# A fused attention and feed-forward block in fp32: the first feed-forward product with its rows on partitions, in place of transposes of them

## The reference, cut to what matters

```python
# x: (8, 1024, 256); every product in fp32
xn = _layernorm(x)
x_proj = silu(xn @ W1 + b1); u, v, q, k = split(x_proj, 4)        # after a second layer norm of xn
attn = silu(einsum(q, k)) / S                                     # 16 heads of 16
y = _layernorm(av * u, gamma, beta) @ W2 + b2
h = layer_norm(xn, ln1_g, ln1_b)                                  # 256 wide
h = einsum('bsd,hd->bsh', h, ternary_quant(w1)) + b1              # 1024 wide
h = layer_norm(gelu(h), ln2_g, ln2_b)
out = einsum('bsh,dh->bsd', h, ternary_quant(w2)) + b2
return x + y + out
```

## Time and profile before

| | us |
|---|---|
| median of 3 executions | 1493.01 (1492.65 to 1493.11) |
| the profiled execution | 1493.36 |
| its span, first to last instruction | 1491.6 |
| one batch, start to start | 181 |
| TensorE busy | 1464.8 (98%) |
| ScalarE busy | 1208.9 (81%) |
| VectorE busy | 895.3 (60%) |
| GpSimd busy | 97.4 (7%) |
| granted TensorE clock | 0.997 of full |

### The profile page before, as it was taken

One profiled execution on the slowest core, in us unless ns is written; L12 is line 12 of the kernel. 1 busy time (PEld: TensorE's weight loads), 2 busy tenths in 40 slices (PEclk: granted clock), 3 DMA queues, 4 the chain that ended last, 5 costly groups with the idle time before them and its releaser, 6 DMA issues.

```text
span 1491.6 us, 25963 instructions
## 1 busy us (share of the span) xinstructions
PE 1464.8 (98%) x9942; PEld 784.7 (53%) x9942; DVE 895.3 (60%) x1719; ACT 1208.9 (81%) x1273; POOL 97.4 (7%) x197
## 2 busy tenths in 40 slices
PE   8999999999999999999999999999999999999998
PEld 7445555455554555554554455545555455554544
DVE  5557655576546854468654685447755476545745
ACT  4788888888788887887878878788788887888885
POOL 2001000010000100001000010000100001000001
PEclk9999999999999999999999999999999999999999
DMA  7351052410524106340153402443033510435100
GB/s 248 81 128 57 15 132 65 130 57 15 156 71 100 58 15 156 95 104 29 30 155 99 113 1 59 126 129 84 1 89 110 142 57 5 115 81 142 29 1 29
DMA packets 67996, 123.49 MB, mean 83 GB/s; under 512 B 12832, under 2 KB 14496, under 8 KB 66976
## 3 DMA queue, kind: packets, MB, share of 16 engines
q1 hardware_dynamic: 67712, 121.57, 29.9%
q10 hardware_dynamic: 160, 0.26, 0.1%
HBM read 79.84 MB, written 41.94 MB: 82 GB/s over the span
## 4 chain that ended last, share of the span: by engine, by line
PE 88%; DVE 5%; ACT 4%; issue 1%; DVEq 1%; DMA 0%; ACTq 0%
PE outs L1101 30%; PE scores L1079 22%; PE fill L1136 10%; PE fill L1170 9%; PE fill L1154 7%; PE fill L1186 3%; PE fill L1163 3%; ACT attn L636 3%; PE fill L1145 2%; DVE tmp L917 1%; PE fill L1126 1%; DVE hid L900 1%; ACT hid L681 1%; DVE st L813 1%; ACT L636 1%
## 5 line engine op out<-in xcount | busy, mean ns | idle before, releaser
L636 ACT ACTIVATE attn<-scores 128x1024 f32<-128x1024 f32 x1024 | 991.4, 1023 | 225.3 <-PE scores L1079 220.6
L1101 PE MATMUL outs<-attn,V 128*32 128x512 f32 x4096 | 494.3, 600 | 0.0
L1079 PE MATMUL scores<-QS,KS 64*128 64x512 f32 x2048 | 387.7, 452 | 8.3 <-ACT attn L636 7.0
L1079 PEld LDWEIGHTS scores<-QS,KS 64*128 64x128 f32 x2048 | 163.0, 184 | 300.4 <-ACT attn L636 241.5
L1101 PEld LDWEIGHTS outs<-attn,V 128*32 128x32 f32 x4096 | 107.2, 109 | 235.8 <-issue 235.1
L900 DVE SCALAR_TENSOR_TENSOR hid<-fill,ratq,fb1b 128x512 f32<-128x512 f32 x128 | 96.1, 751 | 77.6 <-PE fill L1154 72.3
L917 DVE TENSOR_TENSOR tmp<-fill,l2g 128x512 f32<-128x512 f32 x128 | 88.6, 692 | 88.6 <-PE fill L1163 81.1
L1170 PE MATMUL fill<-Wq,hgh 128*128 128x256 f32 x504 | 128.2, 292 | 2.0 <-DVE hgl L924 1.1
L1136 PE MATMUL fill<-xp,W1h 128*128 128x512 f32 x384 | 128.4, 416 | 0.5 <-DVE xp L949 0.5
L1170 PE MATMUL fill<-Wq,hgl 128*128 128x256 f32 x504 | 123.1, 282 | 0.0
L1170 PEld LDWEIGHTS fill<-Wq,hgh 128*128 128x128 f32 x504 | 95.8, 190 | 18.9 <-issue 14.6
(11 more groups left out here) (138 smaller groups left out, 1349.3 us busy)
## 6 DMA issues: line engine op xcount, KB each, us to landing
QS<-q_scratch SPq DMA_DIRECT2D x254, 128.0 KB, 3.3
k_scratch<-kst SPq DMA_DIRECT2D x64, 256.0 KB
q_scratch<-qst SPq DMA_DIRECT2D x64, 256.0 KB
KS<-k_scratch SPq DMA_DIRECT2D x128, 128.0 KB, 3.2
KS<-k_scratch SPq DMA_DIRECT2D x256, 64.0 KB, 3.4
out_dram<-part SPq DMA_DIRECT2D x15, 512.0 KB, 2.6
xin<-in_x SPq DMA_DIRECT2D x7, 1024.0 KB, 5.1
xin<-in_x SPq DMA_DIRECT2D x2, 512.0 KB, 4.3
```

What stands on the lines that cost most here:

```text
L636: nc.scalar.activation(attn_of(g)[:, 2 * hf:2 * hf + 2, :], SP[:, 2 * hf:2 * hf + 2, :], ACT.Silu).then_inc(s_silu, 1)
L1079: ins = mm(SP[:, j, :], KS[rows, pair, t * P:(t + 1) * P], QS[rows, pair - c * PPC, h * HALF:(h + 1) * HALF], start=True, stop=True)
L1101: ins = mm(OP[32 * j:32 * j + 32, g // RUN % 2, :], V[:, t, c * HPC // 2 + j, o * DH:o * DH + 2 * DH], attn_of(g)[:, n, :], start=(o == 0 ...
```

## The change: what it does

1. **f1** is now `f1.h.c`, half of the tokens (512) by 128 of the 1024 hidden features. The stationary operand is a 128x128 piece of `Wq1`, the moving operand a pair of y (256 columns), so a step has 8 matmuls of 256 columns in place of 4 of 512. The product has the hidden features on partitions and the tokens along the row, as f2 wants them. The bias is a value per partition; the ratio per token can't be, so it is multiplied into y before.
2. That ratio has to lie along a row in every partition: SP writes it to DRAM (`write_ratio`) and loads it broadcast (`load_ratio`), and `y` waits for it.
3. The transposes `g` (128 in all, of four instructions), the norming `nrm2` and the moments `ln2` are gone. `hg.t.r` multiplies, rounds and subtracts as `g` did, out of SBUF.
4. The second layer norm is taken out of the product. Sums and sums of squares over the features are needed: in `sum.i` GpSimd squares and adds the 8 feature tiles of a pair (15 instructions of 128x256); the plain sum is made by VectorE in one tensor_reduce for pairs 0 and 1, and by GpSimd with 7 more instructions for pairs 2 and 3. `ts.i`: TensorE adds over the partitions with 4 fp32 matmuls of 2 columns, VectorE makes mean and variance (4 small instructions), GpSimd the root and its product with the mean (2 instructions). In `f2` VectorE adds mean times a constant row `gwb` (one more instruction) and then the product times the root.
5. **TABLE** and `LAST_ROUNDS` are made anew; the load of the next x comes earlier on SP's queue, after `px` instead of after f1; `gelu.0` and `gelu.1` lie side by side, and `gelu.2` and `gelu.3`.
6. The preparation has a product for `gwb` (8 matmul calls) and one for the bias column (24 small ones) in place of two for a bias row.

```diff
 TABLE (rounds 12 to 31, two rows joined to one round)
+12  f1.0.3 | f1.0.4 gelu.0 f1.0.5 f1.0.6 f1.0.7 f1.1.0 f1.1.1 f1.1.2 gelu.1 hg.0.0 hg.0.1
+13  sum.0 | f1.1.3
+14  f1.1.4 f1.1.5 f1.1.6 f1.1.7 | ts.0 sum.1 f2.0 gelu.2 gelu.3 hg.1.0
+15  | hg.1.1
+16  xn.0 f2.1 hg.2.0 xt.0 xn.1 | hg.2.1
+17  ts.1 xt.1 |
+18  | f2.2
+19  | hg.3.0 k.0.0 hg.3.1 xn.2
+20  q.0.0 | sum.2
+21  f2.3 | hg.4.0 hg.4.1
+22  | ts.2 sum.3 xt.2
+23  f2.4 hg.5.0 hg.5.1 |
+24  xn.3 v.0 |
+25  v.1 |
+26  v.2 xt.3 |
+27  f2.5 |
+28  hg.6.0 hg.6.1 k.0.1 | ts.3
+29  f2.6 | hg.7.0
+30  v.3 hg.7.1 |
+31  q.0.1 | f2.7 vs.0
...
 SP, body(b)
+                    load_ratio(b)
...
+                    if h == 0 and b < NB - 1:
+                        sp.wait_ge(s_px, b + 1)
+                        load_x(b + 1)
...
-                    wait_evacuated(sp, b, ("f1", T - 3, 1))
-                    load_x(b + 1)
+                    write_ratio(b + 1)
...
 GpSimd
+                elif kind == "sum":
+                    i = a[0]
+                    pool.wait_ge(s_gelu, NP * x + i // 2 * 2 + 2)
+                    if x or i:
+                        wait_filled(pool, *((x, ("ts", i - 1)) if i else (x - 1, ("ts", NP - 1))))
+                    rows = hid_pair(i)
+                    nc.gpsimd.tensor_tensor(acc[:, 1, :], rows[:, 0, :], rows[:, 0, :], ALU.mult)
+                    if i not in SUMMED_BY_DVE:
+                        nc.gpsimd.tensor_tensor(acc[:, 0, :], rows[:, 0, :], rows[:, 1, :], ALU.add)
+                    for c in range(1, HC):
+                        nc.gpsimd.tensor_tensor(sq[:, :], rows[:, c, :], rows[:, c, :], ALU.mult)
+                        if i not in SUMMED_BY_DVE and c > 1:
+                            nc.gpsimd.tensor_tensor(acc[:, 0, :], acc[:, 0, :], rows[:, c, :], ALU.add)
+                        pool.drain()
+                        ins = nc.gpsimd.tensor_tensor(acc[:, 1, :], acc[:, 1, :], sq[:, :], ALU.add)
+                        pool.drain()
+                    ins.then_inc(s_sq, 1)
...
 VectorE
+                        V_.tensor_reduce(acc[:, 0, :], hid_pair(i).rearrange("p c n -> p n c"), mybir.AxisListType.X,
+                                         ALU.add).then_inc(s_sum, 1)
...
                     V_.tensor_tensor(tmp[:, :].rearrange("p (c n) -> p c n", n=P),
-                                     FP[:, k, :].rearrange("p (c n) -> p c n", n=P),
+                                     hid_pair(t // 2)[:, 4 * r:4 * r + 4, t % 2 * P:(t % 2 + 1) * P],
                                      l2g[:, 4 * r:4 * r + 4].unsqueeze(2).broadcast_to([P, 4, P]), ALU.mult)
...
                 elif kind == "f2":
                     t = a[0]
+                    dve.wait_ge(s_rs2, NP * x + t // 2 + 1)
+                    V_.scalar_tensor_tensor(out=part[:, t, :], in0=gwb[:, :], scalar=nm2[:, t:t + 1],
+                                            in1=part[:, t, :], op0=ALU.mult, op1=ALU.add)
...
 TensorE
-                    passes = [(part, kc) for kc in range(DC) for part in range(2)]
-                    for n, (part, kc) in enumerate(passes):
-                        ins = mm(bank, y_of(t // 2)[:, part, kc, t % 2 * P:(t % 2 + 1) * P], Wq1[:, kc, hf * HALF:(hf + 1) * HALF],
-                                 start=n == 0, stop=n == len(passes) - 1)
-                elif kind == "g":
...
+                    passes = [(kc, part) for kc in range(DC) for part in range(2)]
+                    for i in range(2):
+                        for n, (kc, part) in enumerate(passes):
+                            ins = mm(bank[:, i * PAIR:(i + 1) * PAIR], Wq1[:, kc, c * P:(c + 1) * P],
+                                     y_of(2 * h + i)[:, part, kc, :], start=n == 0, stop=n == len(passes) - 1)
+                elif kind == "ts":
+                    i = a[0]
+                    if i in SUMMED_BY_DVE:
+                        pe.wait_ge(s_sum, len(SUMMED_BY_DVE) * x + SUMMED_BY_DVE.index(i) + 1)
+                    pe.wait_ge(s_sq, NP * x + i + 1)
+                    for n in range(2):
+                        for j in range(2):
+                            col = 4 * n + 2 * j
+                            ins = mm(bank[:, col:col + 2], acc[:, n, j * P:(j + 1) * P], mean_of[:, :],
+                                     start=True, stop=True)
```

More of the change, by code:

```diff
@@ L77 @@
     "",
-    "",
-    "k.1.1",
-    "q.1.1",
-    "",
[L82 to L96, removed]
+    "u.1.1 y.1",
+    "k.1.1 y.0",
+    "ln1 y.2",
+    "q.1.1",
+    "u.0.1",
+    "u.1.0",
+    "f1.0.0 y.3",
+    "",
+    "f1.0.1 f1.0.2",
+    "f1.0.3",
+    "f1.0.4 gelu.0 f1.0.5 f1.0.6 f1.0.7 f1.1.0 f1.1.1 f1.1.2 gelu.1 hg.0.0 hg.0.1",
+    "sum.0",
+    "f1.1.3",
+    "f1.1.4 f1.1.5 f1.1.6 f1.1.7",
+    "ts.0 sum.1 f2.0 gelu.2 gelu.3 hg.1.0",
+    "",
+    "hg.1.1",
+    "xn.0 f2.1 hg.2.0 xt.0 xn.1",
+    "hg.2.1",
+    "ts.1 xt.1",
     "",
     "",
-    "ln1 g.2.1 f1.7.1",
+    "f2.2",
     "",
[L101 to L104, removed]
-    "",
-    "g.4.0 g.4.1",
-    "xt.1",
-    "xn.2 f2.4 xt.2",
-    "",
-    "k.0.0",
-    "g.5.0",
-    "g.5.1 gelu.3 v.0 xn.3 v.1",
+    "hg.3.0 k.0.0 hg.3.1 xn.2",
+    "q.0.0",
+    "sum.2",
+    "f2.3",
+    "hg.4.0 hg.4.1",
+    "",
+    "ts.2 sum.3 xt.2",
+    "f2.4 hg.5.0 hg.5.1",
+    "",
+    "xn.3 v.0",
+    "",
+    "v.1",
+    "",
+    "v.2 xt.3",
+    "",
     "f2.5",
[L114 to L117, removed]
-    "",
-    "k.0.1 g.6.1",
-    "q.0.1",
[L121 to L125, removed]
+    "",
+    "hg.6.0 hg.6.1 k.0.1",
+    "ts.3",
+    "f2.6",
+    "hg.7.0",
+    "v.3 hg.7.1",
+    "",
+    "q.0.1",
+    "f2.7 vs.0",
 )
@@ L138 @@
 LAST_ROUNDS = {
[L139 to L150, removed]
+    16: "f2.1 hg.2.0 hg.2.1",
+    17: "ts.1",
+    18: "f2.2",
+    19: "hg.3.0 hg.3.1",
+    20: "sum.2",
+    21: "f2.3 hg.4.0 hg.4.1",
+    22: "ts.2 sum.3",
+    23: "f2.4 hg.5.0 hg.5.1",
+    24: "",
+    25: "zs.0 zt.0 zt.1",
+    26: "a.0",
+    27: "f2.5 zs.1",
+    28: "hg.6.0 hg.6.1 ts.3 a.1",
+    29: "f2.6 hg.7.0",
+    30: "hg.7.1",
     31: "",
@@ L439, in last_z @@
         def last_z(i, part, c):
-            return yX[:, i, part, c, :]
+            return y01[:, i, part, c, :]
         def last_uz(i, c):
@@ L544, in _ @@
                 load_k(0, 0, h, o)
+            write_ratio(0)
             load_q(0, 0, 0, 1)
@@ L547, in _ @@
                 load_q(0, 0, 1, o)
+            load_ratio(0)
             for b in range(NB):
@@ L601, in step @@
             def step(x, kind, *a):
-                if kind in ("zt", "ln2", "ln1"):
+                if kind in ("zt", "sum", "ts", "ln1"):
                     pool.drain()
@@ L769, in setup_scales @@
                 V_.reciprocal(cq[:, :], scl[:, :])
+                dve.drain()
             def setup_ternary(raw, q, scale):
@@ L1023, in finish @@
                     dve.drain()
+                dve.wait_ge(s_rs2, NP * NB)
+                V_.scalar_tensor_tensor(out=part[:, T - 1, :], in0=gwb[:, :], scalar=nm2[:, T - 1:T],
+                                        in1=part[:, T - 1, :], op0=ALU.mult, op1=ALU.add)
+                dve.drain()
                 dve.wait_ge(s_last_f2, 1)
-                V_.scalar_tensor_tensor(out=part[:, T - 1, :], in0=OP[:, 0, 0:D], scalar=cq[:, 1:2],
+                V_.scalar_tensor_tensor(out=part[:, T - 1, :], in0=OP[:, 0, 0:D], scalar=rs2[:, T - 1:T],
                                         in1=part[:, T - 1, :], op0=ALU.mult, op1=ALU.add)
```

288 lines of the change are left out of this document (171 added, 117 removed).

## The result

The changed kernel takes **1532.34 us**, median of 4 runs (1529.31 to 1535.34), beside 1492.85 for the kernel before, run again on the same chip: a ratio of 1.0264, 95% interval 1.0237 to 1.0292. It is slower, by 39 us; the profiled execution took 1529.31, its span 1527.2, its mean clock 0.985 (before 0.997). Faster, 1487, was forecast, and the range ended at 1530.

The account below looks back on a forecast made before the run. TensorE, busy 98% of the span, was taken to set the pace almost everywhere. Transposes, f1, ts, preparation and GpSimd's stall summed as 1493.4 - 72 + 0 + 34 + 6 + 26 = 1487 us, range 1455 to 1530.

Parts of the forecast that it names:

- The transposes: TensorE's 128 transposing steps go, with their waits for VectorE: -72 us, between ends of 52 and 78.
- f1's own price: TensorE's f1 with 8 matmuls of 256 columns in place of 4 of 512: +0 us, between -9 and +15.
- ts: TensorE's new step, 4 calls of two fp32 passes each, 32 times: +34 us, lower end 17.
- GpSimd is in time: Rival, chance 0.27: GpSimd's sums never hold TensorE, 0 for the stall and 7 gained for ScalarE: 1468 us.
- the part on GpSimd: TensorE waits before ts for GpSimd's sums, 1.8, 1.4 and 0 us, 3.2 a batch: +26 us.
- the reduce: VectorE's tensor_reduce of 2048 elements, two a batch: 2.3 us each, by the row L875.
- VectorE's sum per batch: VectorE's work falls from 110 to some 105 us of 175; worst round 8, 11.8 us of work in 4.8, costed at nothing.
- ScalarE's 7 us: TensorE waits for ScalarE around rounds 13 and 15, 0.9 us a batch, 7 in all, inside the stall in round 14.
- Sums hold TensorE at ts: Slower rival, chance 0.37: GpSimd's sums hold TensorE at ts.0, ts.1 and ts.2, 7.5 us a batch (1521) to 18 (1607).
- by half its length: Within the slower case: each overlapping VectorE instruction delays GpSimd by half its length; stalls 2.4, 3.5, 1.6, 7.5 a batch, 1521 us.
- the fourth: Rival: VectorE, late from waiting for GpSimd, holds f1's banks in round 14, so TensorE waits; counted with the slower case.
- the slower case: Rival, chance 0.37: GpSimd's sums hold TensorE before ts, above 4.0 us a batch the change loses; 1521 to 1607 us.

Follow-up runs that it names:

- the third kernel: The changed kernel with nearly all of GpSimd's sums left out and VectorE's tensor_reduce of pairs 0 and 1 replaced by a copy of one tile: 1478.23 us.

## Why the prediction was wrong

**Right.** The transposes were priced at -72 and gave -74.2. f1's own price, +0: without its waits it takes 134.1 (in the third kernel) against 135.3 before. The preparation was priced at +6 and takes 8 us more than before. ts was priced at +34 and stands at 33.9, but that is luck: its eight passes cost less than forecast, 29.7 us in the third kernel, and some 4 us of waits stand on top, its own and that of the `xt` behind it. GpSimd's means, 0.70 and 0.81 us, lie below and inside the 0.73 to 0.95 named. Without the waits the sum would be the rival "GpSimd is in time", 1468; the kernel with neither part measured 1478. The scores alone are 9 us above their 7 there, and the other terms, too high and too low by 1 to 4 us, nearly cancel.

**The step that failed** is in the part on GpSimd: "What one costs GpSimd isn't shown for long operations", and the stall was then put on GpSimd alone, at ts (1.8, 1.4 and 0 us, +26 in all). The slowing works both ways. The earlier trace rows showed GpSimd waiting for VectorE, and I carried over that direction only: hg stayed "at 0.69 + 0.43 + 0.69", though my estimate of GpSimd's loss itself speaks of a VectorE instruction "that had to wait". Measured, hg takes 0.84 + 0.60 + 0.88, half a us more each time, 128 times, and without GpSimd's sums exactly the old durations. The wait at ts came to 0.9 us in place of 26; with the reduce left out, and VectorE's delay with it, it was 7.6. The Trainium skill, page "SBUF — State Buffer", section "Who interferes with whom", says that whoever starts first has the pair for the whole instruction and the other blocks; I named both directions and priced only GpSimd's. The runs agree: above, GpSimd's sum that starts at 676.24 ends at 677.39, and VectorE's rounding that starts at 676.86, 0.43 us long when alone, ends at 677.66, 0.27 after it, which is near to a full block. They agree also where it sets no block: the reduce and GpSimd's squares run beside each other at their own lengths.

**A term mis-sized**: the reduce, "2.3 each by L875, the nearest row of that length". It measured 3.84 here and 2.29 with neighbouring elements. The row had the right length and the wrong access. These 1.55 us, twice a batch, are worth 25 us.

**A conclusion that didn't follow**: VectorE's sum per batch went down on my paper (110 to 105), and I looked for its worst round by counting work at the old durations, and found round 8. I costed this at nothing. The full stretch is 12 to 16, where hg.0, the first reduce, five evacuations, the second reduce, hg.1 and xn follow each other. The change had brought gelu, hg, sum and f1 into one stretch, and I had checked its windows for GpSimd only. In the batch from 822 to 1003 us VectorE is busy 119.4 of 181, not 105; 8 of the 14 are hg's, 3 the reduces'.

**Slips in the sum.** For ts.0 the prediction has 12.1 us of time and 12.9 of work, which lacks 0.8 us and not 0.6. For ts.1 the rival "by half its length" gives 8.2 / 2 - 1.2 = 2.9 and not 3.5, so 6.9 a batch and 1517 in place of 1521. Neither changes the outcome.

**ScalarE's 7 us** were to be swallowed by the stall in round 14. They measured 16 and were not swallowed: the scores wait the same 16.0 to 16.1 us in the changed kernel, without GpSimd's sums and without either part, and by starts they take 16 us more than before in the last of these. ScalarE in that third kernel, and TensorE beside it:

```profile
663.31 1.28 ACT L747 ACT_TABLE_LOAD   x1
664.61 3.83 ACT L747 ACTIVATE hid<-hid 128x2048 f32<-128x2048 f32 x2
668.46 1.28 ACT L702 ACT_TABLE_LOAD   x1
669.75 5.73 ACT L702 ACTIVATE attn<-scores 128x1024 f32<-128x1024 f32 x6
```

```profile
672.87 0.50 PE L1171 MATMUL scores<-QS,KS 64*128 64x512 f32 x2 [0.64 <-ACT attn L702]
673.70 0.50 PE L1171 MATMUL scores<-QS,KS 64*128 64x512 f32 x2 [0.32 <-ACT attn L702]
```

ScalarE has no pause from 663.31 to 675.48, and TensorE waits 0.96 us for it: the 0.9 us a batch of the prediction were right as a wait, and wrong in being swallowed. Why the last batch and rounds 15 and 16 cost more than that by starts was not taken apart by an experiment.

**The rivals.** "Sums hold TensorE at ts" had the sign right and the place wrong; it came about only in the kernel with all sums on GpSimd, which gave 1602 with 83 us of waits at ts. What happened is the fourth, "VectorE, late from its own waits for GpSimd, holds f1's banks in round 14", which I counted in with the slower case and gave no time; the waits are for f1's banks as it says. With its measured terms on the undisturbed 1468 (25 for f1, that is 2.3 us of wait a batch and mostly lower clock for the rest; 18 for f2, 7 of them its waits for hg and 8 the wait of the `xt` that follows it for xn; 11 more at the scores; 4 in times_v) it gives 1526. That is an account made afterwards, not a forecast.
